# Low parts of the hidden layer's weights: six subtractions moved from GpSimd to VectorE's loop over the tiles of nodes

## The chip, the cores and the metric

The kernel runs on one core of one Trainium2 chip. The metric is the device time of one execution in microseconds (us). In the names of the profile, PE is TensorE, DVE is VectorE, ACT is ScalarE, POOL is GpSimd, and SP is SyncE, which issues the transfers here.

## The reference, cut to what matters

One layer of a graph network on 1250 nodes with 768 features. The stage in question normalizes x and computes the first ("hidden") layer of the graph part:

```python
xn = _layernorm(x, axis=-1)                      # x: (1250, 768)
x1 = jax.nn.relu(xn @ W_ah + b_ah)               # W_ah: (768, 768)
xs = [jax.nn.relu(gat_conv(x1, src, dst, W, a_s, a_d, b)) for W, a_s, a_d, b in ...]   # three graph convolutions
x = x + graph_part(xn) + linear_attention(xn)    # then a feed-forward part with four experts
```

All matmuls are made in split precision: each operand is the sum of a rounded high part and a low part, and a product takes three matmuls: high by high, high by low, and low by high.

## The kernel before, in words

The program has four stages: `front`, `attention`, `projection`, `convolutions`. Each engine has an instruction list of its own, written out by hand in program order; engines wait for each other by semaphores. The change is in `front`, which fills the first 130 us or so.

**Tiles of nodes.** The 1250 nodes are ten tiles of 125 (t = 0 to 9). For a tile, VectorE takes statistics (`statistics`, L334 to L337), ScalarE the deviation (L446), VectorE the reciprocal (L355) and the normalized rows `xN` (L356). TensorE turns the tile in six transposes (`turn_x`, L530), in two halves of three. ScalarE copies each half out of PSUM as the high part `xnh` (L466), and VectorE subtracts it from PSUM to get the low part `xnl` (`low_part`, L344). VectorE's loop over t is a software pipeline: step t holds the statistics of tile t + 1, then the two low parts of tile t - 1, then the reciprocal and the scaling of tile t. So the scaling of tile t stands behind the low parts of tile t - 1.

**The hidden layer.** W_ah comes in six blocks o = 0 to 5 of 128 columns (`w_raw[o]`), loaded by SP. ScalarE makes `w_high[o]` (L450, `high_part(o)`) in its own step t = o + 2, behind the two copies of `xnh` for tile t; the semaphore is `high_ready`. The low part `w_low[o]` overwrites `w_raw[o]`; its semaphore is `low_ready`. TensorE computes `hidden(i)` for 18 pairs of a chunk of nodes (418, 416, 416) and a block o: 18 matmuls each (lines L101 to L103). For the first chunk, `hidden(o)` waits for `low_ready` at o + 1; `hidden(0)` also waits for the first eight low parts of x, which VectorE ends in its step 4. TensorE's order is: turns 0 to 3, `hidden(0)`, turn 4, `hidden(1)`, turn 5, `hidden(2)`, and so on to turn 9, then `hidden(6)` to `hidden(17)`.

**Behind it.** After its loop VectorE computes the reach of each window of edges (L374 to L389), then 96 small products and sums for the attention vectors (L401). TensorE needs them once `hidden(17)` is done (L585). The scores and the counting of edges (L627) follow, and then the other stages.

GpSimd makes constants at the start, has the six subtractions (L321), and then waits for the scores (L324).

Of the kernel before, what the change touches and what calls it, by code (L numbers as in the profile page):

```python
# [19 lines left out]
F32 = mybir.dt.float32  # L20
# [6 lines left out]
ALU = mybir.AluOpType  # L27
# [7 lines left out]
KT = D // 128  # L35
# [136 lines left out]
def front(nc, g):  # L172
# [3 lines left out]
    with ExitStack() as ctx:  # L176
# [23 lines left out]
        w_high = [at(f"wah_high{o}", WS + 3072 * o, [128, KT, 128], F32R) for o in range(KT)]  # L200
        w_raw = [at(f"wah_raw{o}", WS + 3072 * (KT + o), [128, KT, 128]) for o in range(KT)]
        w_low = [at(f"wah_low{o}", WS + 3072 * (KT + o), [128, KT, 128], F32R) for o in range(KT)]
# [104 lines left out]
        @block.gpsimd  # L307
        def _(pool):
            own = Counter(pool, pool_own)
            nc.gpsimd.iota(node_i[:, :], pattern=[[1, N]], base=0, channel_multiplier=0).then_inc(const_ready, 1)  # L310
            nc.gpsimd.iota(start_i[:, :], pattern=[[0, 1]], base=0, channel_multiplier=P).then_inc(const_ready, 1)
            nc.gpsimd.iota(unit_no_i[:, :], pattern=[[1, ET]], base=0, channel_multiplier=0).then_inc(const_ready, 1)
            own.done(nc.gpsimd.memset(ident[:, :], 0.0))
            own.done(nc.gpsimd.affine_select(out=ident[:, :], in_=ident[:, :], compare_op=ALU.not_equal, fill=1.0,
                                             base=0, pattern=[[-1, 128]], channel_multiplier=1))
            nc.gpsimd.memset(ones[:, :], 1.0).then_inc(const_ready, 1)
            own.done(nc.gpsimd.memset(eye[:, :], 0.0))
            nc.gpsimd.tensor_copy(eye[:, N - P:N], ident[0:P, 0:P]).then_inc(const_ready, 1)
            for o in range(KT):
                pool.wait_ge(high_ready, o + 1)  # L320
                nc.gpsimd.tensor_tensor(w_low[o][:, :, :], w_raw[o][:, :, :], w_high[o][:, :, :].bitcast(F32),  # L321
                                        ALU.subtract).then_inc(low_ready, 1)
            pool.wait_ge(ab_taken, 1)
            own.done(nc.gpsimd.tensor_copy(acol[:, :, :], ab[:, :, 0:HEADS].rearrange("p t h -> p h t")))  # L324
            own.done(nc.gpsimd.tensor_scalar(ncol[:, :, :], acol[:, :, :], SLOPE - 1.0, None, ALU.mult))

        @block.vector
        def _(dve):
# [3 lines left out]
            def statistics(t):  # L332
                dve.wait_ge(x_in[t % 6], 32 * (t // 6 + 1))
                nc.vector.bn_stats(stats[:, t % 2, 0, :], xN[:, t, 0:D // 2]).then_inc(dve_own, 1)  # L334
                own.n += 1
                own.done(nc.vector.bn_stats(stats[:, t % 2, 1, :], xN[:, t, D // 2:D]))
                nc.vector.bn_aggr(moments[:, t, :], stats[:, t % 2, :, :]).then_inc(var_ready, 1)  # L337

            def low_part(i):

                t, half = i // 2, i % 2
                dve.wait_ge(xt_free, i + 1)
                part = (slice(None), slice(3 * half, 3 * half + 3), slice(t * P, (t + 1) * P))
                nc.vector.tensor_tensor(xnl[part], bank(i % 4)[:, 0:3 * P].rearrange("p (k n) -> p k n", k=3),  # L344
                                        xnh[part].bitcast(F32), ALU.subtract).then_inc(xl_ready, 1)

            statistics(0)
            for t in range(NT):
                if t + 1 < NT:
                    statistics(t + 1)  # L350
                if t >= 1:
                    low_part(2 * t - 2)
                    low_part(2 * t - 1)
                dve.wait_ge(std_ready, t + 1)
                own.done(nc.vector.reciprocal(rstd[:, t:t + 1], std[:, t:t + 1]))  # L355
                nc.vector.tensor_scalar(xN[:, t, :], xN[:, t, :], moments[:, t, 0:1], rstd[:, t:t + 1],  # L356
                                        ALU.subtract, ALU.mult).then_inc(xn_ready, 1)
                if t == 1:
                    dve.wait_ge(const_ready, 5)
                    own.done(nc.vector.tensor_copy(node_id[:, :], node_i[:, :]))  # L360
                if t == 6:
                    dve.wait_ge(edges_in, 48)
                    own.done(nc.vector.tensor_copy(chunk_f[:, :], chunk_i[:, :]))
                    own.done(nc.vector.tensor_copy(src_f[:, 0:ET], src_i[:, :]))
                    own.done(nc.vector.tensor_copy(dst_f[:, 0:ET], dst_i[:, :]))
                    own.done(nc.vector.memset(src_f[:, ET:ET + CE - 1], 0.0))
                    own.done(nc.vector.memset(dst_f[:, ET:ET + CE - 1], -1.0))
                    units_of = chunk_f[:, :].rearrange("c (u p) -> c u p", u=2)
                    own.done(nc.vector.tensor_reduce(ends[:, 0, :], units_of, axis=AX.X, op=ALU.min))
                    nc.vector.tensor_reduce(ends[:, 1, :], units_of, axis=AX.X, op=ALU.max).then_inc(ends_ready, 1)  # L370
# [65 lines left out]
            for k, (_, t0, n) in enumerate(TURNS):  # L436
                dve.wait_ge(turn_full, len(TURNS) * (NT - 1) + k + 1)
                nc.vector.tensor_copy(cnt[:, t0:t0 + n, (NT - 1) * P:NT * P],
                                      bank(k)[0:P, 0:P * n].rearrange("p (t n) -> p t n", t=n)).then_inc(turn_free, 1)
# [1456 lines left out]
```

## Time and profile before

| | |
|---|---|
| time, median of 3 runs | 1415.84 us (1415.65 to 1416.47) |
| the profiled execution's own time | 1416.86 us |
| its span, first to last instruction | 1414.9 us |
| TensorE busy | 1355.7 us, 96% |
| VectorE busy | 1047.7 us, 74% |
| ScalarE busy | 500.8 us, 35% |
| GpSimd busy | 41.3 us, 3% |
| mean granted clock of TensorE | 0.989 |

The execution's own time is 1.96 us above its span: what lies around the first and last instruction. Rows of the timeline give the start and duration in us, the engine, the line of the kernel, what was done, and in brackets how long the engine had been idle before it and what ended that. Durations of neighbours on one engine overlap slightly, so distances are best taken from start to start.

### The profile page before, as it was taken

The numbers are of one execution on the slowest core, as the hardware profiler recorded it, in microseconds if no ns is written. First come the engines' busy times: TensorE is split into PE (matmuls) and PEld (weight loads), VectorE is DVE, ScalarE is ACT, GpSimd is POOL, SyncE is SP. The second block draws the span as 40 slices with busy tenths as digits, with TensorE's granted clock in tenths as the row PEclk, the third lists the DMA queues.
The fourth block names the chain that finished last, engine by engine and source line by source line (L and its number), as shares of the span: only waits on it lengthen the run. The fifth ranks groups of instructions, "written<-read, shape, count | busy, mean of one in ns | idle before, by whom it ended". The sixth has DMA issues, their size and how long they took to land.

```text
span 1414.9 us, 21075 instructions
## 1 busy us (share of the span) xinstructions
PE 1355.7 (96%) x8144; PEld 1267.2 (90%) x8144; DVE 1047.7 (74%) x1927; ACT 500.8 (35%) x820; POOL 41.3 (3%) x43
## 2 busy tenths in 40 slices
PE   5999999999999799999999999999999999999897
PEld 4964566999999799999999999999999999999885
DVE  6867988799999842686676677676757766768667
ACT  3211134334334511444333433343243324333373
POOL 3100000000000050000000000000000000000000
PEclk9999999999999899999999999999999999999998
DMA  9310000221221574511101110111012011104003
GB/s 292 104 68 2 0 1 3 87 89 71 89 89 38 180 218 160 138 37 37 39 1 71 37 40 1 70 37 40 1 70 76 1 70 37 42 1 137 7 1 109
DMA packets 23619, 91.59 MB, mean 65 GB/s; under 512 B 3681, under 2 KB 4864, under 8 KB 20589
## 3 DMA queue, kind: packets, MB, share of 16 engines
q1 hardware_dynamic: 22609, 88.07, 19.2%
q10 hardware_dynamic: 924, 2.30, 0.6%
q8 instruction: 62, 1.02, 0.3%
q14 instruction: 24, 0.20, 0.0%
HBM read 79.30 MB, written 11.06 MB: 64 GB/s over the span
## 4 chain that ended last, share of the span: by engine, by line
PE 53%; DVE 6%; ACT 1%; issue 1%; DVEq 0%
PE psum L1699 25%; PE psum L101 8%; PE psum L102 8%; PE psum L103 8%; DVE hN L1323 1%; PE psum L1713 1%; DVE prob L1307 1%; DVE prob L1301 1%; PE psum L1753 1%; DVE acc L1345 0%; DVE x1l L1330 0%; PE psum L1768 0%; ACT prob L1529 0%; DVE acc L1361 0%; DVE xll L1336 0%
## 5 line engine op out<-in xcount | busy, mean ns | idle before, releaser
L1699 PE MATMUL psum<-hN,prob 125*125 125x193 f32 x2400 | 409.0, 327 | 1.5 <-DVE hN L1323 1.5
L1699 PEld LDWEIGHTS psum<-hN,prob 125*125 125x125 f32 x2400 | 395.4, 187 | 2.0 <-issue 1.8
L1529 ACT ACTIVATE prob<-prob,acol 125x1250 f32<-125x1250 f32 x120 | 160.9, 1341 | 381.5 <-DVE prob L1301 381.5
L1307 DVE SCALAR_TENSOR_TENSOR prob<-prob,cnt 125x1250 f32<-125x1250 f32 x120 | 174.7, 1456 | 56.3 <-ACT prob L1529 56.3
L1301 DVE SCALAR_TENSOR_TENSOR prob<-vrow,ncol,urow 125x1250 f32<-125x1250 f32 x120 | 182.0, 1516 | 9.5 <-PE psum L1699 9.5
L742 DVE CUSTOM_DVE_ANT_0 junk<-mask,arow 125x1250 bf16<-125x1250 uint8 x120 | 174.8, 1457 | 3.1
L101 PE MATMUL psum<-woh,xlh 128*125 128x384 f32 x360 | 127.2, 353 | 2.6 <-DVE acc L1345 2.6
L101 PE MATMUL psum<-wph,x1h 128*125 128x384 f32 x330 | 118.4, 359 | 4.8 <-PEq L958 1.9
L102 PE MATMUL psum<-wol,xlh 128*125 128x384 f32 x360 | 122.6, 340 | 0.0
L103 PE MATMUL psum<-woh,xll 128*125 128x384 f32 x360 | 121.9, 339 | 0.0
L103 PE MATMUL psum<-wph,x1l 128*125 128x384 f32 x330 | 111.9, 339 | 0.0
L102 PE MATMUL psum<-wpl,x1h 128*125 128x384 f32 x330 | 111.9, 339 | 0.0
L627 PE MATMUL psum<-hot_src,hot_dst 125*125 125x418 bf16 x540 | 110.5, 355 | 0.8 <-DVE hot_src L429 0.8
L101 PE MATMUL psum<-wq_high,xnh 128*125 128x256 f32 x360 | 103.0, 286 | 1.3 <-PEq L176 1.3
L627 PEld LDWEIGHTS psum<-hot_src,hot_dst 125*125 125x125 bf16 x540 | 60.9, 136 | 47.5 <-DVE hot_src L429 38.8
L102 PE MATMUL psum<-wq_low,xnh 128*125 128x256 f32 x360 | 101.6, 282 | 0.0
L103 PE MATMUL psum<-wq_high,xnl 128*125 128x256 f32 x360 | 101.5, 282 | 0.0
L429 DVE TENSOR_SCALAR hot_src<-node_id,src_f 125x1250 bf16<-125x1250 f16 x180 | 97.7, 543 | 0.0
L1330 DVE TENSOR_TENSOR x1l<-x1T,x1h 128x750 fp32r<-128x750 f32 x54 | 50.8, 941 | 60.0 <-ACT x1h L1537 59.3
L1336 DVE SCALAR_TENSOR_TENSOR xll<-psum,xlh 128x375 fp32r<-128x375 f32 x60 | 32.8, 547 | 80.9 <-ACT xlh L1548 80.9
L1537 ACT ACTIVATE x1h<-x1T 128x750 fp32r<-128x750 f32 x54 | 44.9, 831 | 73.7 <-PE psum L103 73.7
L101 PEld LDWEIGHTS psum<-woh,xlh 128*125 128x125 f32 x360 | 67.2, 187 | 4.1 <-issue 3.9
(241 smaller groups left out, 2216.4 us busy)
## 6 DMA issues: line engine op xcount, KB each, us to landing
arow<-scratch_a SPq DMA_DIRECT2D x12, 625.0 KB, 4.0
urow<-scratch_uv SPq DMA_DIRECT2D x12, 625.0 KB, 4.1
vrow<-scratch_uv SPq DMA_DIRECT2D x12, 625.0 KB, 5.7
wq_raw<-in_w_qkv SPq DMA_DIRECT2D x6, 1152.0 KB, 6.7
wp_raw<-in_w_pair SPq DMA_DIRECT2D x6, 1152.0 KB, 7.5
wo_raw<-in_w_out SPq DMA_DIRECT2D x6, 1152.0 KB, 5.1
wl<-in_w_gat SPq DMA_DIRECT2D x4, 1152.0 KB, 11.0
xN<-in_x SPq DMA_DIRECT2D x10, 336.0 KB
```

The source lines that it names most:

```text
L101: nc.tensor.matmul(psum, s_high, m_high, start=first, stop=False)
L102: nc.tensor.matmul(psum, s_high, m_low, start=False, stop=False)
L103: return nc.tensor.matmul(psum, s_low, m_high, start=False, stop=last)
L429: nc.vector.tensor_scalar(hot_src[:, e, :], node_id[:, :], src_f[:, bass.ds(unit + e, 1)], None, ALU.is_equal).then_inc(hot_ready, 1)
L627: last = nc.tensor.matmul(at_window(w, c)[0:P, 0:n], hot_dst[:, e, 0:P], hot_src[:, e, c0:c0 + n], start=False, stop=False, skip_group_che ...
L742: own.done(nc.vector.tensor_tensor_reduce(out=junk[:, :], in0=mask[:, t, :], in1=arow[head % 2][0:P, :], scale=1.0, scalar=0.0, op0=ALU.mu ...
L1301: nc.vector.scalar_tensor_tensor(prob[n % RING][:, :], vrow[head % 2][0:P, :], ncol[:, head, j:j + 1], urow[head % 2][0:P, :], op0=ALU.add ...
L1307: nc.vector.scalar_tensor_tensor(prob[n % RING][:, :], prob[n % RING][:, :], 1.0, cnt[:, n % NT, :], op0=ALU.min, op1=ALU.mult).then_inc(p ...
L1330: nc.vector.tensor_tensor(low[:, :, :], x1T[:, :, t * P:(t + 1) * P], high[:, :, :].bitcast(F32), ALU.subtract)\
L1529: nc.scalar.activation(prob[n % RING][:, :], prob[n % RING][:, :], ACT.Exp, bias=acol[:, n // NT, n % NT:n % NT + 1]).then_inc(e_ready, 1)
L1537: nc.scalar.activation(x1_parts(i, t)[0][:, :, :], x1T[:, :, t * P:(t + 1) * P], ACT.Copy).then_inc(xh_ready, 1)
L1699: last = nc.tensor.matmul(bank(t // 2)[0:P, 193 * (t % 2):193 * (t % 2) + 193], ring[:, t * P:(t + 1) * P], hN[i % 2][:, j, 193 * s:193 * ...
```

## The change

The loop of six subtractions leaves GpSimd's list. A function `hidden_weights_low(o)` with the same subtraction and the same semaphores is added to VectorE's list, and called at the end of VectorE's steps t = 2 to 7 (the third to the eighth tile), for o = t - 2. In step 6 it stands ahead of the casts of the edge lists. Nothing changes for TensorE, ScalarE and SP. The six instructions have the same operands and shape (128 partitions by 768, 32 bit).

```diff
             nc.gpsimd.tensor_copy(eye[:, N - P:N], ident[0:P, 0:P]).then_inc(const_ready, 1)
-            for o in range(KT):
-                pool.wait_ge(high_ready, o + 1)
-                nc.gpsimd.tensor_tensor(w_low[o][:, :, :], w_raw[o][:, :, :], w_high[o][:, :, :].bitcast(F32),
-                                        ALU.subtract).then_inc(low_ready, 1)
             pool.wait_ge(ab_taken, 1)
...
+
+            def hidden_weights_low(o):
+                dve.wait_ge(high_ready, o + 1)
+                nc.vector.tensor_tensor(w_low[o][:, :, :], w_raw[o][:, :, :], w_high[o][:, :, :].bitcast(F32),
+                                        ALU.subtract).then_inc(low_ready, 1)
...
                 nc.vector.tensor_scalar(xN[:, t, :], xN[:, t, :], moments[:, t, 0:1], rstd[:, t:t + 1],
                                         ALU.subtract, ALU.mult).then_inc(xn_ready, 1)
+                if 2 <= t < 2 + KT:
+                    hidden_weights_low(t - 2)
```

VectorE's list before, from the scaling of tile 2 to the scaling of tile 4 (steps 3 and 4 of the loop), with the semaphore that each instruction waits for:

```order
L356 TENSOR_SCALAR xN<-xN,moments,rstd 125x768 [waits dve_own]
L334 BN_STATS stats<-xN 125x6 [waits x_in4]
L336 BN_STATS stats<-xN 125x6
L337 BN_AGGR moments<-stats 125x2 [waits dve_own]
L344 TENSOR_TENSOR xnl<-psum,xnh 128x3x125 [waits xt_free] x2
L355 RECIPROCAL rstd<-std 125x1 [waits std_ready]
L356 TENSOR_SCALAR xN<-xN,moments,rstd 125x768 [waits dve_own]
L334 BN_STATS stats<-xN 125x6 [waits x_in5]
```

The same place in the changed kernel, whose lines are numbered anew (L357 is the scaling, L345 the moved subtraction, L330 to L333 the statistics, L340 the low parts of x):

```order
L357 TENSOR_SCALAR xN<-xN,moments,rstd 125x768 [waits dve_own]
L345 TENSOR_TENSOR wah_low_95<-wah_raw_89,wah_high_83 128x768 [waits high_ready]
L330 BN_STATS stats<-xN 125x6 [waits x_in4]
L332 BN_STATS stats<-xN 125x6
L333 BN_AGGR moments<-stats 125x2 [waits dve_own]
L340 TENSOR_TENSOR xnl<-psum,xnh 128x3x125 [waits xt_free] x2
L356 RECIPROCAL rstd<-std 125x1 [waits std_ready]
L357 TENSOR_SCALAR xN<-xN,moments,rstd 125x768 [waits dve_own]
L345 TENSOR_TENSOR wah_low_96<-wah_raw_90,wah_high_84 128x768 [waits high_ready]
L330 BN_STATS stats<-xN 125x6 [waits x_in5]
```

Between each scaling and the next statistics there is now a subtraction that waits for `high_ready`; it recurs up to the step of tile 7.

GpSimd's list before, from its last constants on:

```order
L317 MEMSET eye 125x2375
L318 CAST eye<-ident 125x125 [waits pool_own]
L321 TENSOR_TENSOR wah_low_95<-wah_raw_89,wah_high_83 128x768 [waits high_ready]
L321 TENSOR_TENSOR wah_low_96<-wah_raw_90,wah_high_84 128x768 [waits high_ready]
L321 TENSOR_TENSOR wah_low_97<-wah_raw_91,wah_high_85 128x768 [waits high_ready]
L321 TENSOR_TENSOR wah_low_98<-wah_raw_92,wah_high_86 128x768 [waits high_ready]
L321 TENSOR_TENSOR wah_low_99<-wah_raw_93,wah_high_87 128x768 [waits high_ready]
L321 TENSOR_TENSOR wah_low_100<-wah_raw_94,wah_high_88 128x768 [waits high_ready]
L324 COPY acol<-ab 125x120 [waits ab_taken]
```

The same place in the changed kernel:

```order
L314 AFFINE_SELECT ident<-ident 128x128 [waits pool_own]
L316 MEMSET ones 128x64 [waits pool_own]
L317 MEMSET eye 125x2375
L318 CAST eye<-ident 125x125 [waits pool_own]
L320 COPY acol<-ab 125x120 [waits ab_taken]
```

The six subtractions are gone from it, and it goes from the constants straight to the wait for the scores.

## Rows read from the trace of the kernel before

**Rows 1.** The page, part 1: busy us, share of the span, instructions.
```profile
PE 1355.7 (96%) x8144; PEld 1267.2 (90%) x8144; DVE 1047.7 (74%) x1927; ACT 500.8 (35%) x820; POOL 41.3 (3%) x43
```
**Rows 2.** Timeline of all engines, 14 to 22 us: tiles 2 to 4.
```profile
14.69 0.68 DVE L356 TENSOR_SCALAR xN<-xN,moments,rstd 125x768 f32<-125x768 f32 x1
...
15.43 1.51 PE L530 MATMUL psum<-ident,xN 125*128 125x125 f32 x6 [2.15 <-DVE xN L356]
...
17.36 0.83 ACT L450 ACTIVATE wah_high<-wah_raw 128x768 fp32r<-128x768 f32 x1
...
18.15 0.68 DVE L356 TENSOR_SCALAR xN<-xN,moments,rstd 125x768 f32<-125x768 f32 x1
...
21.60 0.68 DVE L356 TENSOR_SCALAR xN<-xN,moments,rstd 125x768 f32<-125x768 f32 x1
...
21.64 0.69 PE L101 MATMUL psum<-xnh,wah_high 128*128 128x418 f32 x1 [1.25 <-DVE xnl L344]
```
**Rows 3.** Timeline of all engines, 27 to 47 us: tiles 4 to 8.
```profile
27.76 0.80 PE L530 MATMUL psum<-ident,xN 125*128 125x125 f32 x6
...
28.80 1.00 DVE L344 TENSOR_TENSOR xnl<-psum,xnh 128x375 fp32r<-128x375 f32 x2 [5.35 <-ACT xnh L466]
...
29.03 0.85 ACT L450 ACTIVATE wah_high<-wah_raw 128x768 fp32r<-128x768 f32 x1
...
29.91 2.30 DVE L356 TENSOR_SCALAR xN<-xN,moments,rstd 125x768 f32<-125x768 f32 x1
...
29.95 1.84 POOL L321 TENSOR_TENSOR wah_low<-wah_raw,wah_high 128x768 fp32r<-128x768 f32 x1 [5.99 <-ACT wah_high L450]
...
32.14 0.55 DVE L334 BATCH_NORM_STATS2 stats<-xN 125x6 f32<-125x384 f32 x1
...
32.27 0.86 PE L530 MATMUL psum<-ident,xN 125*128 125x125 f32 x6 [0.29 <-DVE xN L356]
...
33.37 1.00 DVE L344 TENSOR_TENSOR xnl<-psum,xnh 128x375 fp32r<-128x375 f32 x2
...
34.48 2.31 DVE L356 TENSOR_SCALAR xN<-xN,moments,rstd 125x768 f32<-125x768 f32 x1
...
36.71 0.28 DVE L363 CAST chunk_f<-chunk_i 80x250 f32<-80x250 int32 x1
...
36.85 0.86 PE L530 MATMUL psum<-ident,xN 125*128 125x125 f32 x6 [0.28 <-DVE xN L356]
...
38.61 0.55 DVE L334 BATCH_NORM_STATS2 stats<-xN 125x6 f32<-125x384 f32 x1
...
41.56 0.86 PE L530 MATMUL psum<-ident,xN 125*128 125x125 f32 x6 [0.44 <-DVE xN L356]
...
46.14 0.86 PE L530 MATMUL psum<-ident,xN 125*128 125x125 f32 x6 [0.28 <-DVE xN L356]
```
**Rows 4.** The page, part 5: VectorE's nearest subtraction, busy us, mean ns | idle.
```profile
L1330 DVE TENSOR_TENSOR x1l<-x1T,x1h 128x750 fp32r<-128x750 f32 x54 | 50.8, 941 | 60.0 <-ACT x1h L1537 59.3
```
**Rows 5.** Busy us by stretch: PE, PEld, DVE, ACT, POOL, PEclk, DMA, GB/s.
```profile
51.00:101.00 50.00, 49.73 (x247) 42.67 (x245) 39.12 (x207) 9.02 (x18) 0.00 (x0) 1.00 0.27 96
```
**Rows 6.** Timeline, end of VectorE's products, and TensorE's first use of them.
```profile
93.78 0.36 DVE L401 CUSTOM_DVE_ANT_0 prod<-wl,a_bc 128x192 f32<-128x192 f32 x1
...
101.43 12.77 PE L585 MATMUL psum<-x1T,wa 128*24 128x418 f32 x36 [0.70 <-ACT x1T L455]
```
**Rows 7.** Timeline of TensorE in the last stage: two waits.
```profile
1370.56 0.54 PE L1779 MATMUL psum<-ident,comb 125*128 125x125 f32 x3 [1.66 <-DVE comb L1418]
...
1379.97 0.44 PE L1797 MATMUL psum<-wu_high,full_parts 128*125 128x384 f32 x1 [1.46 <-DVE full_parts L1433]
```
**Rows 8.** Busy us by stretch around the first wait; columns as in rows 5.
```profile
1371.00:1372.00 1.00, 0.98 (x5) 0.50 (x4) 0.93 (x1) 0.39 (x1) 0.00 (x0) 1.00 0.00 0
1372.00:1373.00 1.00, 0.89 (x3) 0.62 (x4) 0.96 (x3) 0.39 (x1) 0.00 (x0) 0.62 0.00 0
1373.00:1375.00 2.00, 2.00 (x9) 2.00 (x8) 0.29 (x2) 1.53 (x3) 0.00 (x0) 0.50 0.00 0
1376.00:1377.00 1.00, 1.00 (x8) 1.00 (x7) 0.97 (x4) 0.64 (x1) 0.00 (x0) 1.00 0.00 0
```

## Prediction

> **What bounds the kernel now.** I read the page first, then the timeline of the first 130 us, then the stretches. TensorE is busy for 96% of the span [rows 1], so the first question for any edit is whether TensorE will wait longer. The change lies in the first 50 us. The timeline shows two regimes there. Up to 21.6 us TensorE has only the turns of tiles, and waits for the scaling of each: 2.15 us ahead of turn 2 [rows 2]. The loop "scaling of tile t, turn, copies of `xnh`, low parts, scaling of tile t + 1" sets the pace, one step in 3.45 us (18.15 to 21.60) [rows 2]. `hidden(0)` starts at 21.64, released by the low parts of x [rows 2]. From then on TensorE has a turn and a `hidden` per step, and it sets the pace: the turns start at 27.76, 32.27, 36.85, 41.56 and 46.14, with waits of only 0.29, 0.28, 0.44 and 0.28 us ahead of the last four, 1.29 us in all [rows 3]. After that it is busy for 49.73 of 50 us [rows 5]. So whatever delays turn 8 delays everything behind it.
>
> The row to look at is the one of GpSimd: its subtraction starts 0.07 us after the end of ScalarE's high part (29.03 + 0.85 = 29.88, then 29.95) [rows 3]. It is fed as early as it can be, and waits on an engine that has nothing else to do. The question is what the same wait does on VectorE.
>
> **The change part by part.** *Removed:* six subtractions on GpSimd, 1.84 us in the hot part [rows 3]. They run over VectorE's scaling: that one lasts 2.30 and 2.31 us where the same instruction takes 0.68 us elsewhere [rows 2, 3]. In the trace three of the scalings (tiles 5, 6 and 8) are that long. What this costs TensorE is no more than its four short waits, 1.29 us; the chain below contains no such scaling, so that gain is in the sum already.
>
> This fits what the Trainium skill states (SBUF — State Buffer, "SBUF: two separate sides"): VectorE and GpSimd share a port pair under an exclusive lock, and the loser waits for the whole instruction. By that rule alone the change would be a gain of those 1.29 us, which is a rival below.
>
> *Added:* six subtractions on VectorE. The nearest row is a subtraction of 128 by 750 with the same types, 0.941 us [rows 4]; 941 x 768 / 750 = 0.96 us. The next instruction on VectorE starts about 0.08 us before such a row ends (29.91 + 2.30 = 32.21 against 32.14) [rows 3], so I take 0.88 us. Bounds: 0.68 us, the one-input instruction of the same width [rows 2], and 1.84 us, GpSimd's own [rows 3]; the value lies at VectorE's own subtraction, since it is the same operation on the same engine.
>
> *The wait, which is the larger part.* The subtraction for o = t - 2 stands behind the scaling of tile t and waits for the high part that ScalarE makes in its step t, behind its copies of tile t, and those need the turn of tile t, which needs that very scaling. So VectorE always arrives too early, by a whole round over TensorE and ScalarE. Behind it are queued the statistics of tile t + 1, which could have run in that time, the low parts of x, and the next scaling, for which TensorE waits. Before, VectorE's statistics ran inside that round; now they stand behind it. VectorE doesn't pass by a waiting instruction: in the gap of 5.35 us ahead of 28.80 it ran nothing [rows 3].
>
> The length of a step in the new order, start to start:
> - scaling to turn: 14.69 to 15.43 = 0.74 [rows 2];
> - turn to the end of the high part: with TensorE at 1.2 GHz 17.36 + 0.83 - 15.43 = 2.76 [rows 2], with it at 2.4 GHz 29.88 - 27.76 = 2.12 [rows 3]; the six transposes take 1.51 us in the one case and 0.80 in the other;
> - to the start of the subtraction: 0.07, as for GpSimd;
> - subtraction: 0.88;
> - statistics to low parts: 32.14 to 33.37 = 1.23 [rows 3];
> - low parts to scaling: 33.37 to 34.48 = 1.11 [rows 3].
>
> That is 6.79 us for a slow step and 6.15 us for a fast one. Counted on from tile 2's scaling at 14.69: tile 3 at 21.48 (18.15 before), tile 4 at 28.27 (21.60 before). `hidden(0)` starts 0.04 us behind that, at 28.31: 6.67 us late. It then runs as before, so turn 4 comes 27.76 - 21.64 = 6.12 us later, at 34.43. Turns 5 and 6 follow after 6.15 us each: 40.58 and 46.73. Step 6 has the casts of the edge lists behind the subtraction as well (36.71 to 38.61 = 1.90) [rows 3], so turn 7 comes at 46.73 + 6.15 + 1.90 = 54.78, and turn 8 at 60.93 against 46.14: **14.8 us late**. TensorE's work from turn to turn is 32.27 - 0.29 - 27.76 = 4.22 us, so it now waits 1.9 us three times and 3.8 us once. Turn 9 has no subtraction ahead of it: step 9 hides behind `hidden(5)` as before.
>
> *Behind the front.* Nothing takes the 14.8 us back. VectorE's work after its loop moves by the same amount. Its 96 products end at about 94.1 and are first needed at 101.43, where TensorE waited 0.70 us for ScalarE's copy of x1 [rows 6]. Both move together, and the cover of 7.3 us stays. Transfers: those of SP for this stage are issued ahead of the loop or behind signals that move along; I cost them at nothing.
>
> *TensorE's clock.* A stretch with such waits can cost clock. In the last stage a wait of 1.66 us ended at 1370.56 [rows 7]; the granted clock was 1.00 at 1371, 0.62 in the next us, 0.50 (1.2 of 2.4 GHz) to 1375, and 1.00 again in the us from 1376 [rows 8]. After the wait of 1.46 us that ended at 1379.97 [rows 7] it stayed at 1.00. So waits of 1.9 and 3.8 us may or may not bring a fall. Its price: a slow turn adds 2.76 - 2.12 = 0.64 us to a step; slow matmuls first use up TensorE's wait. A wholly slow step is TensorE's own 6.12 + 1.2 (a turn: 0.56 fast, plus 1.51 - 0.86) = 7.3 us instead of 6.15, or 1.15 more. I take one fall or two, 1.0 us in all; bounds 0, and 3 x 1.15 + 0.64 = 4.1 us, plus some 1.2 us if the matmuls behind turn 8 are slow as well.
>
> **The rivals.**
> - *Clock down through most of the stretch:* 14.8 + 4.1 + 1.2 = 20.1 us more, 1435.9 us. For it: the four waits come one after another. Against it: a TensorE that is slow has no waits left, and its clock came back in rows 8.
> - *Only the start-up pays:* the two slow steps cost 6.7 us, and later ones hide under TensorE's work, 1422.5 us. It would need a fast step of at most 4.22 us; without the wait it would be 0.88 + 1.23 + 1.11 + 0.74 plus the copies, but the wait for the high part is in the order itself.
> - *Not slower:* the wait costs VectorE nothing, and the freed scalings save TensorE 1.29 us, 1414.55 us. The place is the end of each step 2 to 7. It decides if the high part is there when VectorE arrives, which is when the scaling ends; the rows put it 0.74 + 2.76 - 0.68 = 2.8 us later in the steps of tiles 2 and 3, and 2.2 us later in the others. The long gap of 5.35 us ahead of 28.80 [rows 3] speaks for free time on VectorE, but it lies on the wrong side: in front of turn 4's copies, for which the high part is waiting too.
>
> The Trainium skill has one more rule that bears on this (TensorE: Matmul & The Clock Gate, the table's row on queue depth): VectorE's queue is strictly first in, first out. The gap of 5.35 us agrees; by this rule the wait goes onto the path in full.
>
> **How the numbers follow.** The sum is 14.8 + 1.0 = 15.8 us. Against the profiled execution's own time that is 1416.86 + 15.8 = 1432.7; it lay 1.0 us above the median of the runs, so for the median I say 1415.84 + 15.8 = 1431.6 us. Chances: this course 0.80, the clock down through most of it 0.15, only the start-up 0.03, not slower 0.02. The range: at the bottom no loss of clock and `hidden(0)` in fast matmuls (2.5 us less than 14.8, as its 6.12 would become 4.22 - 0.56), 1428.1; at the top 1435.9 less a little of that rival, 1435.5. The subtraction at 0.68 would take six times 0.28, 1.7 us, which stays inside; at 1.84 it would go beyond, and no row of VectorE speaks for that. A measurement of this kernel tells 0.2%, 2.8 us, from no change; slower by more than that holds 0.97, within 0.02, faster 0.01.
>
> **What would show it.** In the profile of the changed kernel: each of the six subtractions on VectorE preceded by a wait of about 2.8 us (two) or 2.2 us (four) for ScalarE's high part; no scaling longer than 0.7 us; `hidden(0)` near 28.3 us; turns 5 to 8 each after a wait of 1.9 us, or 3.8 us for turn 7; turn 8 near 61 us; and the stage behind it the same, shifted by 15 us. I am wrong if VectorE runs past the wait, if the high parts come before the scaling ends, or if `hidden(6)` on is not delayed by what turn 8 is.

## The result and the profile after

The changed kernel takes 1430.65 us (median of 4 runs, 1429.05 to 1434.57), the kernel before next to it 1416.14 us (4 runs). The ratio is 1.0105, with a 95% interval of 1.0093 to 1.0117: 13 to 17 us slower. 1431.6 us was predicted. The profiled execution took 1429.68 us, with a span of 1427.7 us against 1414.9 us.

The page of the changed kernel, part 1, to be held against [rows 1]:

```profile
PE 1354.3 (95%) x8144; PEld 1264.7 (89%) x8144; DVE 1048.6 (73%) x1933; ACT 501.4 (35%) x820; POOL 29.4 (2%) x37
```

VectorE has six instructions more, GpSimd six fewer, and no engine has more work to speak of: VectorE's busy time rises by 0.9 us only, since its three long scalings of [rows 3] are 1.63 us shorter each, which nearly pays for six subtractions of 0.96 us. TensorE's busy time is the same within 1.4 us, its span is 12.8 us longer: it waits.

VectorE in the timeline of the changed kernel (start us, us, engine, line, operation; in brackets the idle time before it and what ended it), tiles 2 and 3, then tiles 5 to 7:

```profile
14.42 0.68 DVE L357 TENSOR_SCALAR xN<-xN,moments,rstd 125x768 f32<-125x768 f32 x1
17.95 0.96 DVE L345 TENSOR_TENSOR wah_low<-wah_raw,wah_high 128x768 fp32r<-128x768 f32 x1 [2.85 <-ACT wah_high L453]
18.82 0.56 DVE L330 BATCH_NORM_STATS2 stats<-xN 125x6 f32<-125x384 f32 x1
...
20.00 0.95 DVE L340 TENSOR_TENSOR xnl<-psum,xnh 128x375 fp32r<-128x375 f32 x2
...
21.05 0.68 DVE L357 TENSOR_SCALAR xN<-xN,moments,rstd 125x768 f32<-125x768 f32 x1
24.58 0.96 DVE L345 TENSOR_TENSOR wah_low<-wah_raw,wah_high 128x768 fp32r<-128x768 f32 x1 [2.85 <-ACT wah_high L453]
...
36.13 0.96 DVE L345 TENSOR_TENSOR wah_low<-wah_raw,wah_high 128x768 fp32r<-128x768 f32 x1 [7.76 <-ACT wah_high L453]
...
42.16 0.96 DVE L345 TENSOR_TENSOR wah_low<-wah_raw,wah_high 128x768 fp32r<-128x768 f32 x1 [2.26 <-ACT wah_high L453]
...
48.20 0.96 DVE L345 TENSOR_TENSOR wah_low<-wah_raw,wah_high 128x768 fp32r<-128x768 f32 x1 [2.25 <-ACT wah_high L453]
49.07 0.28 DVE L366 CAST chunk_f<-chunk_i 80x250 f32<-80x250 int32 x1
```

Every subtraction has a wait for ScalarE's high part ahead of it, which before lay on GpSimd (the sixth, at 56.46 us, one of 2.59 us). The scaling follows only after the subtraction, the statistics and the low parts. From scaling to scaling it is 21.05 - 14.42 = 6.63 us, against 3.45 us in [rows 2].

TensorE in the same timeline: `hidden(0)`, then turns 4 to 8, to be held against [rows 2, 3]:

```profile
27.73 0.69 PE L101 MATMUL psum<-xnh,wah_high 128*128 128x418 f32 x1 [4.43 <-DVE xnl L340]
...
33.98 0.80 PE L533 MATMUL psum<-ident,xN 125*128 125x125 f32 x6
39.96 0.86 PE L533 MATMUL psum<-ident,xN 125*128 125x125 f32 x6 [1.76 <-DVE xN L357]
46.00 0.86 PE L533 MATMUL psum<-ident,xN 125*128 125x125 f32 x6 [1.74 <-DVE xN L357]
53.93 1.25 PE L533 MATMUL psum<-ident,xN 125*128 125x125 f32 x6 [3.65 <-DVE xN L357]
60.30 0.86 PE L533 MATMUL psum<-ident,xN 125*128 125x125 f32 x6 [0.50 <-DVE xN L357]
```

`hidden(0)` is 6.09 us late, turn 4 6.22, turn 5 7.69, turn 6 9.15, turn 7 12.37 and turn 8 14.16 us. Where the clock fell, the stretches show (busy us and count of PE, PEld, DVE, ACT, POOL, then the granted clock of TensorE as a share of 2.4 GHz, so that 0.50 is 1.2 GHz, DMA share and GB/s):

```profile
50.00:54.00 4.00, 0.34 (x3) 0.07 (x2) 3.67 (x11) 0.29 (x1) 0.00 (x0) 1.00 0.02 0
54.00:55.00 1.00, 1.00 (x7) 1.00 (x8) 0.00 (x0) 0.41 (x1) 0.00 (x0) 0.63 0.00 0
55.00:57.00 2.00, 2.00 (x7) 1.92 (x7) 0.54 (x1) 1.79 (x4) 0.00 (x0) 0.50 0.49 12
58.00:59.00 1.00, 1.00 (x7) 0.99 (x6) 0.97 (x4) 0.29 (x1) 0.00 (x0) 1.00 0.00 0
```

TensorE had 0.34 us of work in the four us before the fall, the wait for turn 7 that the casts lengthen. Behind it turn 7 took 1.25 us, and TensorE's own slow matmuls used up most of the next wait, which is 0.50 us.

The line behind the hidden layer, TensorE's products with the attention vectors, answers to [rows 6]:

```profile
L588 PE MATMUL psum<-x1T,wa x36: 510/512/532, 115.6 to 127.9; 128*24 128x416 f32 x24, 128*24 128x418 f32 x12
```

The first starts at 115.6 us against 101.43: the 14.2 us of turn 8, nothing gained or lost in between.

### The profile page after: what moved, and what is told of

Its sections match the earlier page's. It is cut to its first block, busy times and chain, and to the rows that moved or that the text cites. A ratio compares the mean times of both kernels' runs of the same rounds, so it can differ in the third digit from the quotient of the medians.

```text
span 1427.7 us, 21075 instructions
## 1 busy us (share of the span) xinstructions
PE 1354.3 (95%) x8144; PEld 1264.7 (89%) x8144; DVE 1048.6 (73%) x1933; ACT 501.4 (35%) x820; POOL 29.4 (2%) x37
## 4 chain that ended last, share of the span: by engine, by line
PE 52%; DVE 7%; ACT 1%; issue 1%; DVEq 0%
PE psum L1702 25%; PE psum L101 8%; PE psum L102 8%; PE psum L103 8%; DVE hN L1326 1%; PE psum L1716 1%; DVE prob L1310 1%; DVE prob L1304 1%; PE psum L1756 1%; DVE acc L1348 0%; DVE x1l L1333 0%; DVE acc L1364 0%; DVE acc L1443 0%; ACT prob L1532 0%; PE psum L1771 0%
```

## The experiments

All edits are to the changed kernel, unless the text says otherwise. Ratios are to the kernel before on the same chip. Over the two sessions that kernel spread from 1413.61 to 1419.5 us (21 runs) and from 1413.72 to 1418.86 us (13 runs), wider than its first three runs; what the clock has to do with it is told further down.

**Each subtraction one step later.**

```diff
-                if 2 <= t < 2 + KT:
-                    hidden_weights_low(t - 2)
+                if 3 <= t < 3 + KT:
+                    hidden_weights_low(t - 3)
```

> The same six subtractions on VectorE, each one step later (block o at the end of the step of tile o + 3), where its high part has long been there. My theory (the wait costs, not the work): no wait ahead of the subtractions, turn 8 near 45 to 46 us, and 1415 us, between the kernel before and 1.3 us under it. Rival (VectorE's added work, 5.3 us in all, is what costs): some 5 us above the kernel before, 1421 us, or still near 1430.

Measured: 1417.24 us (11 runs), ratio 1.0001 (0.9991 to 1.0010). VectorE does the same six subtractions, and the answer by tile for them shows no wait under "its engine sat idle before it" (duration least/median/most in ns):

```profile
L345 DVE TENSOR_TENSOR wah_low<-wah_raw,wah_high x6: 949/952/955, 18.8 to 43.7; 128x768 fp32r<-128x768 f32 x6
its engine sat idle before it (us, times) until:
```

TensorE's turns 7 and 8:

```profile
40.17 0.86 PE L533 MATMUL psum<-ident,xN 125*128 125x125 f32 x6 [0.18 <-DVE xN L357]
44.57 0.80 PE L533 MATMUL psum<-ident,xN 125*128 125x125 f32 x6
```

Where no wait stands ahead of it, the work costs nothing that can be measured: all of the 14 us hang on the wait. Turn 8 is even 1.57 us earlier than before (45 to 46 us expected), but the time isn't: that part of the expectation missed, and is taken up below.

**ScalarE's high parts ahead of its copies.** VectorE's list stays that of the changed kernel.

```diff
+                if 2 <= t < 2 + KT:
+                    high_part(t - 2)
                 for i in (2 * t, 2 * t + 1):
                     act.wait_ge(xt_full, i + 1)
...
-                if 2 <= t < 2 + KT:
-                    high_part(t - 2)
```

> The changed kernel with one move on ScalarE: its high part of the weights stands ahead of its copies of the tile's high parts, so that it needs no turn. My theory: VectorE finds the high part ready, the waits of 2.9 and 2.3 us go, turn 8 near 46 us, 1415 to 1416.5 us. Rival (the place of the subtraction in VectorE's list costs, whoever is ready): no less than 1425 us.

Measured: 1416.47 us (11 runs), ratio 0.9993 (0.9983 to 1.0003). ScalarE makes the high part while TensorE turns the tile, and VectorE runs from the scaling straight into the subtraction:

```profile
14.50 0.68 DVE L357 TENSOR_SCALAR xN<-xN,moments,rstd 125x768 f32<-125x768 f32 x1
15.09 0.95 DVE L345 TENSOR_TENSOR wah_low<-wah_raw,wah_high 128x768 fp32r<-128x768 f32 x1
```

Turn 8 is at 44.00 us, 2 us earlier than expected. So the place in VectorE's list isn't at fault by itself: it is the place together with the producer's. Either move heals the change.

**The wait without the work.** The kernel before, GpSimd subtracting, with one wait added to VectorE.

```diff
                                         ALU.subtract, ALU.mult).then_inc(xn_ready, 1)
+                if 2 <= t < 2 + KT:
+                    dve.wait_ge(high_ready, t - 1)
```

> The kernel before, subtractions on GpSimd, with only the wait for the high part added to VectorE at the end of the steps of tiles 2 to 7. My theory: each step is longer by the round less the work, 6.79 - 0.88 = 5.91 us for the first two and 5.27 us for the next ones: hidden(0) 4.9 us late, turn 8 about 9.5 us late, 1425.5 us, with a fall of the clock possible. Rival (the work costs): no change, 1416 us.

Measured: 1427.29 us (4 runs), ratio 1.0070 (1.0055 to 1.0086), about 10 us slower. The statistics now stand behind the wait:

```profile
18.41 0.56 DVE L334 BATCH_NORM_STATS2 stats<-xN 125x6 f32<-125x384 f32 x1 [2.85 <-ACT wah_high L452]
24.17 0.56 DVE L334 BATCH_NORM_STATS2 stats<-xN 125x6 f32<-125x384 f32 x1 [2.85 <-ACT wah_high L452]
```

The step is 24.17 - 18.41 = 5.76 us (5.91 expected); `hidden(0)` starts at 26.45, 4.81 us late (4.9 expected). Turns 5 and 6 wait 0.89 and 0.88 us, where the changed kernel has 1.76 and 1.74: the difference is the subtraction's 0.87 us. So the work does cost something once it stands behind a wait: 0.87 us in each of six steps, 5.2 us.

Turn 8 is at 56.91 us, 10.77 us late where 9.5 was expected, and the time is 1.8 us above the expectation. Turn 7 comes only after a wait of 4.32 us, because the casts of the edge lists, which now stand behind the wait as well, meet GpSimd's subtraction:

```profile
44.86 1.95 POOL L321 TENSOR_TENSOR wah_low<-wah_raw,wah_high 128x768 fp32r<-128x768 f32 x1 [3.31 <-ACT wah_high L452]
45.14 1.78 DVE L366 CAST src_f<-src_i 125x160 f32<-125x160 int32 x1
```

The same cast takes 0.24 us in the kernel before. These 1.5 us are not the wait's, and behind turn 7 the clock fell (0.50 from 53 to 55 us). Without the 1.5 us turn 8 would be 9.2 us late (an estimate), about two thirds of the changed kernel's 14.16, with no work added to VectorE.

**The casts inside the wait.**

```diff
-                if 2 <= t < 2 + KT:
+                if 2 <= t < 2 + KT and t != 6:
                     hidden_weights_low(t - 2)
...
                     nc.vector.tensor_reduce(ends[:, 1, :], units_of, axis=AX.X, op=ALU.max).then_inc(ends_ready, 1)
+                    hidden_weights_low(t - 2)
```

> The changed kernel with the casts and reductions of the edge lists ahead of the subtraction in the step of tile 6, so that they run in its wait. My theory: 1.9 us less than the changed kernel, turn 7 after a wait of 1.75 us like the others and no fall of the clock there: 1428 us. Rival (the casts had been hidden): no change, 1430 us.

Measured: 1430.53 us (4 runs), ratio 1.0096 (1.0081 to 1.0112), not told apart from the changed kernel. The expected 1428 us was missed, though the profiled execution took 1428.21. In its timeline the mechanism is there:

```profile
47.34 0.96 DVE L345 TENSOR_TENSOR wah_low<-wah_raw,wah_high 128x768 fp32r<-128x768 f32 x1 [0.36 <-ACT wah_high L454]
```
```profile
51.18 0.86 PE L534 MATMUL psum<-ident,xN 125*128 125x125 f32 x6 [1.74 <-DVE xN L357]
57.22 0.86 PE L534 MATMUL psum<-ident,xN 125*128 125x125 f32 x6 [1.76 <-DVE xN L357]
```

The wait shrinks to 0.36 us, turn 7 waits 1.74 us instead of 3.65, and turn 8 comes 3.08 us earlier than in the changed kernel. Of that 0.85 us lies ahead of turn 4 and has nothing to do with the casts (`hidden(0)` reached the 2.4 GHz level sooner), 1.90 us is the casts, and 0.33 us the step behind turn 7 without a fall of the clock. The median of the time doesn't show it, and by the time alone the rival would stand.

**The subtraction behind the statistics.**

```diff
                     statistics(t + 1)
+                if 3 <= t < 3 + KT:
+                    hidden_weights_low(t - 3)
                 if t >= 1:
...
-                if 2 <= t < 2 + KT:
-                    hidden_weights_low(t - 2)
```

> The changed kernel with each subtraction moved behind the statistics of the next step, ahead of the low parts of x: the statistics then run inside the wait. My theory (chain: scaling, turn, copies, high part, subtraction, low parts): 5.56 us for the first two steps and 4.92 us for the next, with 5.7 us for the one with the casts; hidden(0) about 4 us late, turn 8 about 6.3 us late, 1422.5 us. Rival (the wait costs the same wherever it stands): 1430 us.

Measured: 1422.66 us (4 runs), ratio 1.0047 (1.0030 to 1.0064). TensorE's turns 5 to 8:

```profile
36.09 0.86 PE L533 MATMUL psum<-ident,xN 125*128 125x125 f32 x6 [0.64 <-DVE xN L359]
41.00 0.86 PE L533 MATMUL psum<-ident,xN 125*128 125x125 f32 x6 [0.62 <-DVE xN L359]
46.59 0.86 PE L533 MATMUL psum<-ident,xN 125*128 125x125 f32 x6 [1.29 <-DVE xN L359]
51.50 0.86 PE L533 MATMUL psum<-ident,xN 125*128 125x125 f32 x6 [0.64 <-DVE xN L359]
```

The steps are 4.91, 5.59 and 4.91 us; 4.92, 5.7 and 4.92 were expected. `hidden(0)` starts at 25.92, 4.28 us late, and turn 8 is 5.36 us late, 0.9 less than expected, of which 0.8 lies between `hidden(0)` and turn 4 (5.31 us, 6.12 before). What stands behind the wait is what it costs: take the statistics out of there and each step is 1.1 us shorter than in the changed kernel (6.04).

**Waits in the first two steps alone.**

```diff
-                if 2 <= t < 2 + KT:
-                    hidden_weights_low(t - 2)
+                if t in (2, 3):
+                    hidden_weights_low(t - 2)
+                if 5 <= t < 3 + KT:
+                    hidden_weights_low(t - 3)
```

> Blocks 0 and 1 as in the changed kernel (with the wait, ahead of hidden(0)), the others one step later, without a wait. My theory, the terms add up: hidden(0) 6.1 us late as in the changed kernel, then no waits behind it, turn 8 some 4.5 us later than before (6.1 less the 1.6 us that the subtractions without a wait give there), 1420.5 us. Rival (a late hidden(0) alone sets off the later waits): near 1430 us.

Measured: 1423.7 us (4 runs), ratio 1.0042 (1.0026 to 1.0059). Turns 4 to 6 start at 34.47, 38.56 and 42.64 us, one in 4.1 us without a wait, and turn 8 at 51.43, 5.3 us later than before. In this execution turn 1, ahead of any edit, was already 0.96 us later than before (12.72 against 11.76), so about 4.3 us of it are the edit's, for 4.5 expected. The late `hidden(0)` sets off nothing; the parts add up. The median is 3 us over the expectation, more than the timeline of the front accounts for. Its profile has a fall of the clock that the kernel before has not: 0.71 from 120 to 125 us and 0.61 from 125 to 130, which is 3.4 us of work at the full clock (an estimate from the two means). Whether that is the reason in every run wasn't tried.

**High parts first, with GpSimd subtracting.** The ScalarE edit above, made to the kernel before.

> The kernel before (subtractions on GpSimd) with ScalarE's high parts of the weights ahead of its copies. GpSimd then subtracts earlier, while VectorE has its statistics and low parts. If the shared use of memory by GpSimd and VectorE is what made the scalings 2.30 us, they are 0.68 us wherever no subtraction runs, and TensorE's 1.29 us of waits go in part: 1415 to 1416 us. If not: unchanged at 1416 us, with the scalings still long.

Measured: 1416.62 us (10 runs), ratio 1.0000 (0.9989 to 1.0011). The scalings of this kernel, and of the kernel before (ns, least/median/most):

```profile
L356 DVE TENSOR_SCALAR xN<-xN,moments,rstd x10: 679/679/680, 7.7 to 46.4; 125x768 f32<-125x768 f32 x10
```
```profile
L356 DVE TENSOR_SCALAR xN<-xN,moments,rstd x10: 678/680/2314, 7.5 to 48.3; 125x768 f32<-125x768 f32 x10
```

With GpSimd's subtractions moved in time, no scaling is long any more, while GpSimd does the same work. Four of its subtractions begin during a scaling and are themselves longer, 2.05 to 2.21 us; the fourth of them:

```profile
39.51 2.21 POOL L321 TENSOR_TENSOR wah_low<-wah_raw,wah_high 128x768 fp32r<-128x768 f32 x1 [3.83 <-ACT wah_high L450]
```

It took 2.21 us instead of 1.84, with the scaling on VectorE from 39.34 to 40.02. So the 2.30 us of [rows 3] were the overlap with GpSimd. The overlap has not gone altogether: another of the subtractions, from 33.83 to 35.68, now meets a cast, which takes 0.24 us in the kernel before:

```profile
34.01 1.77 DVE L364 CAST src_f<-src_i 125x160 f32<-125x160 int32 x1
```

Turn 7 waits 0.83 us for what stands behind that cast, where it waited 0.44 us before. Turn 8 is at 44.20 us, 1.94 us earlier than before. The median of the time doesn't follow. The one profiled execution does: its span is 1413.2 us against 1414.9, and its clock has no fall near 115 us.

**The changed kernel again.** No edit.

> The changed kernel once more, to see how its time and its clock spread from run to run: 1429 to 1434 us if the falls of the clock in the stage vary, with turn 8 between 60 and 62 us; under 1 us of spread if they don't.

Measured: 1433.33 us (4 runs, 1433.03 to 1433.7), ratio 1.0117 (1.0100 to 1.0134). The expectation fits neither way: these four agree within 0.7 us, but lie 2.7 us above the median of the first four, which spread over 5.5 us. The two intervals of the ratio overlap. Its span is 1431.7 us, 4.0 us above that of the first profile, though turn 8 is at 59.78, 0.52 us earlier. Turn 7 took 1.51 us, all of it at the low clock (0.50 from 53 to 58 us), and turn 8 came 6.86 us behind it, against 6.37 us in the first profile and 6.04 us where no clock fell.

The stretches say where the 4.0 us are. The kernel before, the changed kernel, and the changed kernel again, cut at the same points of the program, to the nearest us (first product with the attention vectors, first attention product, first convolution product, last convolution product, end); of the third, the two stretches in which it differs:

```profile
0.00:101.00 101.00, 83.81 (x414) 73.31 (x414) 74.52 (x284) 28.02 (x59) 16.44 (x18) 1.00 0.48 151
101.00:246.00 145.00, 140.96 (x726) 82.17 (x726) 118.75 (x367) 42.27 (x73) 1.21 (x2) 1.00 0.03 9
246.00:588.00 342.00, 327.50 (x2252) 322.22 (x2253) 264.88 (x531) 121.60 (x319) 22.31 (x19) 0.98 0.37 117
588.00:1320.00 732.00, 726.61 (x4352) 723.29 (x4352) 521.03 (x580) 259.99 (x282) 1.39 (x4) 1.00 0.13 43
1320.00:1415.00 95.00, 76.79 (x403) 66.25 (x401) 68.53 (x165) 48.92 (x88) 0.00 (x0) 0.92 0.13 41
```
```profile
0.00:115.00 115.00, 85.54 (x414) 74.90 (x414) 74.54 (x290) 28.52 (x59) 4.56 (x12) 0.99 0.42 132
115.00:260.00 145.00, 141.10 (x726) 82.15 (x726) 118.70 (x367) 42.44 (x73) 1.21 (x2) 1.00 0.03 9
260.00:599.00 339.00, 323.38 (x2253) 317.83 (x2254) 266.41 (x532) 121.52 (x319) 22.24 (x19) 0.99 0.37 118
599.00:1331.00 732.00, 726.62 (x4353) 723.26 (x4351) 520.84 (x580) 260.00 (x282) 1.39 (x4) 1.00 0.13 43
1331.00:1428.00 97.00, 77.64 (x402) 66.56 (x400) 68.08 (x165) 48.94 (x88) 0.00 (x0) 0.92 0.13 40
```
```profile
115.00:261.00 146.00, 142.19 (x727) 83.32 (x727) 119.24 (x367) 41.90 (x72) 1.33 (x3) 0.99 0.03 9
261.00:604.00 343.00, 329.38 (x2256) 324.74 (x2257) 266.35 (x531) 121.69 (x319) 22.15 (x19) 0.97 0.36 116
```

The third part, attention and projection, takes 342 us at a clock of 0.98, 339 us at 0.99 and 343 us at 0.97. It has the same instructions in all three. Taken to the tenth of a us, from the first product with the attention vectors to the first convolution product it is 487.0, 483.7 and 488.8 us. So the profile of the changed kernel flattered it: of its 14.2 us, 3.3 were given back there, and 2 lost again at the end. The same holds for the gains: in the kernel with the subtractions one step later, this stretch reads

```profile
115.00:120.00 5.00, 4.22 (x16) 2.80 (x15) 4.26 (x13) 3.12 (x2) 1.08 (x2) 0.66 0.09 12
```

where the kernel before has

```profile
115.00:120.00 5.00, 4.23 (x25) 2.60 (x24) 4.72 (x13) 3.68 (x3) 1.21 (x2) 1.00 0.09 12
```

A mean of 0.66 over 5 us is 3.4 us at half the clock, which loses 1.7 us of work at the full one: about what its front had won, 1.57 us. The kernel with ScalarE's high parts first reads 0.69 there. That this fall is the reason in every run was not tried.

## Why the prediction was right

*What bounds the kernel, and the wait.* Right. VectorE arrives too early at each subtraction, by 2.85 us in the first two steps (2.8 forecast) and by 2.26, 2.25 and 2.59 us in three of the next (2.2 forecast; the third has the low clock). The wait for block 2 is 7.76 us, not 2.2: there turn 4 stands behind all of `hidden(0)`. The chain of the prediction had that order in its sum (turn 4 is counted from `hidden(0)`); its list of what would be seen had not. The experiments separate the parts: the work without the wait costs nothing; the wait without the work costs 10 to 11 us, 1.5 of them a cast that met GpSimd; and the work behind the wait adds 0.87 us a step, as the sum had it.

*The terms.* The subtraction takes 0.958 us and the next instruction starts 0.87 us behind it (0.96 and 0.88 forecast, from a row of another shape). From statistics to low parts it is 1.18 us, where 1.23 was taken, and from low parts to scaling 1.05 for 1.11; a slow step is 6.63 us for 6.79. Two of them, and tile 2's scaling 0.27 us earlier in this execution, make `hidden(0)` 27.73 instead of 28.31. `hidden(0)` to turn 4 took 6.25 us for 6.12, and 5.25 in the other profile of this kernel: the faster `hidden(0)` that the bottom of the range stood for came in part. The steps behind it are 5.98 and 6.04 us for 6.15, the one with the casts 7.93 for 8.05. Turn 8 is 14.16 us late, for 14.8 plus 1.0 for the clock. The waits of 1.9, 1.9 and 3.8 us were 1.76, 1.74 and 3.65; the fourth, 0.50 for 1.9, was used up by TensorE's own slow matmuls.

*The clock.* One fall, at the longest wait, as "one or two" had it. Its price in the front was 6.37 - 6.04 = 0.33 us in one profile and 6.86 - 6.04 = 0.82 us in the other, less than the 1.0 us taken, since TensorE spends its waits on the slow matmuls first. The rival with the clock down in most of the stretch fell: behind the waits of 1.76 and 1.74 us it stayed up. The waits for turn 7, 3.65 and 3.64 us here and 4.32 in the kernel with the wait alone, each came with a fall. The length of a wait alone doesn't decide: 1.66 us in [rows 7] had one.

*Behind the front.* The step that was incomplete: "nothing takes the 14.8 us back". No work or transfer did, and the lateness is the same 14.2 us at 115.6 us. But up to the first convolution product the later stages, with the granted clock at 0.99 and 0.97 where it had been 0.98, took 3.3 us less in one profile and 1.8 us more in the other. The forecast put nothing there. The medians of 1430.65 us and of 1433.33 us in a later session lie on both sides of it, so that it came within 1 us of the first is in part luck; that the loss is some 14 us is not.

*The gain from GpSimd's overlap.* The rival's mechanism is real: no scaling is longer than 0.682 us in the changed kernel, and moving GpSimd's work in time shows that the overlap made them long, as it did a cast (1.77 us for 0.24). The Trainium skill's rule (SBUF — State Buffer, "SBUF: two separate sides"), an exclusive lock on a shared port pair, fits both directions: a scaling of 2.31 us under GpSimd's subtraction, and a subtraction of 2.21 us that began under a scaling. Who came first can't be read from the recorded starts: at 29.91 the scaling's is 0.04 us ahead of the subtraction's [rows 3], and still the scaling is the long one. The overlap was just not what TensorE waited for, beyond 1.29 us.

## What to carry to other kernels

An instruction moved to another engine takes its wait along, and the wait is paid by everything behind it in that engine's list. Before moving one, find when its producer finishes relative to the new neighbour's own round: here the producer stood behind the very instruction that VectorE had just issued, so a wait of 2 to 3 us per step went onto the critical loop, with the moved work behind it, and moving either side by one place took all 14 us back. A wait put in without any work is a test for this, but look at what else it moves: here it pushed a cast under GpSimd's subtraction. Count gains and losses at a point of the program close to the edit, since an effect of 2 us on the whole time drowns in falls of the clock far away from it.

## What was not expected of the hardware

The kernel's spread is larger than its first three runs show (1415.65 to 1416.47 then, 1413.61 to 1419.5 us later), and the mean granted clock goes with it: 0.992 and 0.993 in the three shortest of those 21 runs, 0.988 in the two longest. In which stage they differ is known only for the profiled ones. Three edits that bring turn 8 forward by 1.6 to 2.1 us changed the time by nothing measurable; in the two profiles of VectorE's versions a fall of the clock near 115 us stood against it, and in the profile of GpSimd's, which has no such fall, the gain is there.

The granted clock doesn't tell all. In the changed kernel it reads 1.00 from 30 to 31 us, with four matmuls under way in that us, and 1.00 from 36 to 37 us with seven (in the timeline one starts each 0.35 us in the former and each 0.19 us in the latter):

```profile
30.00:31.00 1.00, 1.00 (x4) 0.95 (x3) 0.00 (x0) 0.00 (x0) 0.00 (x0) 1.00 1.01 424
36.00:37.00 1.00, 1.00 (x7) 0.99 (x6) 0.87 (x1) 0.60 (x2) 0.00 (x0) 1.00 0.00 0
```

In the first 30 us or so of these profiles, the distance of the matmuls shows the level, not the column of the clock. `hidden(0)` reached the high level between 33.4 and 33.8 us in one execution of the changed kernel and between 31.3 and 31.6 us in the other, from the same start at 27.7 us, which alone is 1.0 us at turn 4 (33.98 against 32.97).
